# Local attention layers on one core: inverse norms by logarithm, exponential and one Newton step for two chunks at a time, and the mask added by four 64x64 matmuls

## The reference, cut to what matters

```
def l2norm(t):
    return t / jnp.clip(jnp.linalg.norm(t, axis=-1, keepdims=True), 1e-12)
...
q = l2norm(q) * qs
k = l2norm(k) * ksc
q, k = rotary_xpos(q, k)
...
bq = q.reshape(b, h, w, WINDOW, d) * QK_SCALE          # WINDOW 64, 8 heads of 64
sim = jnp.einsum('bhwid,bhwjd->bhwij', bq, bk)          # bk: this window's and the one before it
mask = (i < j) | (i > j + WINDOW) | (j == -1)
sim = jnp.where(mask, -jnp.finfo(sim.dtype).max, sim)
attn = jax.nn.softmax(sim, axis=-1)
...
x = x + o @ wo
h = ((h - mu) / jnp.sqrt(var + 1e-05) * lg + lb) @ w1 + b1
a, g = jnp.split(h, 2, axis=-1)
x = x + (a * jax.nn.gelu(g, approximate=False)) @ w2 + b2
```

## Time and profile before

| | |
|---|---|
| median of 3 runs (lowest to highest) | 1306.38 us (1305.3 to 1306.8) |
| the profiled execution: time / span | 1305.02 / 1303.2 us |
| stage A, to the first mask matmul | 590.65 us |
| start of the first and of the last of the 64 steps | 590.65 and 1257.25 us |
| busy share PE, DVE, ACT, POOL | 92, 86, 74, 82% |
| mean granted TensorE clock | 0.984 |

### The profile page before, as it was taken

One profiled execution on the slowest core, in us unless ns is written; L12 is line 12 of the kernel. 1 busy time (PEld: TensorE's weight loads), 2 busy tenths in 40 slices (PEclk: granted clock), 3 DMA queues, 4 the chain that ended last, 5 costly groups with the idle time before them and its releaser, 6 DMA issues.

```text
span 1303.2 us, 37200 instructions
## 1 busy us (share of the span) xinstructions
PE 1200.7 (92%) x12352; PEld 984.2 (76%) x12352; DVE 1124.0 (86%) x2210; ACT 958.8 (74%) x1772; POOL 1070.0 (82%) x1431
## 2 busy tenths in 40 slices
PE   3799999999999999977899999999999999999975
PEld 2588888888888888865677777777777777777764
DVE  2799999999999999957888888888888988888873
ACT  3477777777777777655688878888887877787762
POOL 1877777777777777687999999999999999999962
PEclk9799999999999999998999999999999999999998
DMA  6000000000000000001121211112122111111110
GB/s 181 8 12 14 14 14 14 12 12 12 9 11 12 12 8 10 16 7 46 40 48 39 49 42 43 46 46 50 39 53 52 45 50 47 49 48 47 43 35 25
DMA packets 87053, 44.28 MB, mean 34 GB/s; under 512 B 43908, under 2 KB 80048, under 8 KB 86960
## 3 DMA queue, kind: packets, MB, share of 16 engines
q1 hardware_dynamic: 86960, 43.08, 12.9%
HBM read 19.99 MB, written 6.29 MB: 20 GB/s over the span
## 4 chain that ended last, share of the span: by engine, by line
PE 39%; POOL 32%; DVE 14%; issue 11%; SPq 2%; ACT 1%; POOLq 1%; DVEq 0%; DMA 0%; ACTq 0%
POOL rnorm L716 11%; POOL kT L705 9%; PE bank L1415 7%; PE bank L1382 6%; PE bank L1397 6%; POOL probs L766 4%; DVE sums L1083 4%; POOL kT L719 3%; PE bank L1357 3%; DVE probs L1100 2%; PE bank L1426 2%; PE bank L1533 2%; PE bank L1359 2%; PE bank L1512 2%; PE bank L1568 2%
## 5 line engine op out<-in xcount | busy, mean ns | idle before, releaser
L655 POOL TENSOR_TENSOR probs<-probs,coef 128x1024 f32<-128x1024 f32 x128 | 241.0, 1904 | 5.0
L716 POOL TENSOR_TENSOR rnorm<-norm,halves 128x8 f32<-128x8 f32 x128 | 213.8, 1671 | 10.7
L705 POOL TENSOR_TENSOR kT<-qT 128x512 f32<-128x512 f32 x128 | 164.0, 1281 | 7.2 <-DVE qT L1177 7.2
L1091 DVE TENSOR_REDUCE mx<-bank 128x8 f32<-128x512 f32 x256 | 162.8, 678 | 3.9 <-PE bank L1397 3.8
L1100 DVE TENSOR_TENSOR probs<-bank,mx 128x512 f32<-128x512 f32 x256 | 162.1, 675 | 0.1
L849 ACT ACTIVATE probs<-probs 128x1024 f32<-128x1024 f32 x128 | 135.2, 1056 | 35.7 <-DVE probs L1100 33.8
L1083 DVE TENSOR_REDUCE sums<-probs 128x16 f32<-128x1024 f32 x128 | 154.0, 1212 | 6.5 <-ACT probs L849 6.5
L1382 PE MATMUL bank<-ident,probs 128*128 128x128 f32 x1024 | 137.8, 278 | 10.1 <-ACT wT L843 7.4
L719 POOL TENSOR_TENSOR kT<-kT,rnorm 128x512 f32<-128x512 f32 x128 | 133.6, 1044 | 10.0
L843 ACT ACTIVATE wT<-bank 128x512 f32<-128x512 f32 x256 | 137.1, 589 | 0.5 <-PE bank L1382 0.5
L1382 PEld LDWEIGHTS bank<-ident,probs 128*128 128x128 f32 x1024 | 114.2, 142 | 26.0 <-issue 14.2
(11 more groups left out here) (130 smaller groups left out, 3107.8 us busy)
## 6 DMA issues: line engine op xcount, KB each, us to landing
probs<-f_v SPq DMA_DIRECT2D x96, 128.0 KB, 2.3
res<-stage_x SPq DMA_DIRECT2D x48, 128.0 KB, 3.8
xn<-in_x SPq DMA_DIRECT2D x16, 128.0 KB, 2.2
xr<-in_x SPq DMA_DIRECT2D x16, 128.0 KB, 2.1
stage_x<-xo SPq DMA_DIRECT2D x32, 64.0 KB, 1.6
hn<-stage_x SPq DMA_DIRECT2D x32, 64.0 KB
mn<-mid SPq DMA_DIRECT2D x64, 32.0 KB
stage_x<-yo SPq DMA_DIRECT2D x16, 128.0 KB, 2.1
```

Of the source, the lines that this page charges most:

```text
L655: nc.gpsimd.tensor_tensor(out=e[:, :, :, :], in0=e[:, :, :, :], in1=coef[r % 2][:, 2, A_REP * at:A_REP * (at + 1), :].unsqueeze(3).broadca ...
L705: nc.gpsimd.tensor_tensor(out=qk[m][:, :, :], in0=on_self[m % 2][:, :, :], in1=on_partner[m % 2][:, :, :], op=ALU.add).then_inc(added, 1)
L716: nc.gpsimd.tensor_tensor(out=rnorm[:, at], in0=norm2[:, 1, at], in1=halves[:, 0:F_HEADS], op=ALU.pow).then_inc(rnorm_set, 1)
L1091: nc.vector.tensor_reduce(mx[s % 2][:, 2 * k:2 * k + 2, :], banks[2 * (s % 2) + k][:, :].rearrange("p (h c k) -> p h c k", h=2, c=CHUNKS), ...
```

## The change

The inverse norm is made in another way, on other engines and for two chunks (128x16) at once. ACT squares 2x instead of x, so that the sum is four times the squared norm s. POOL guards it, once for two chunks. ACT takes Ln, then Exp with a scale of -0.5: an r near s^-0.5. POOL makes one Newton step of four small operations, (3 - s r r) r, and multiplies both chunks one after the other. ACT's table loads are written out by hand: one set that holds both functions is loaded at the start of the step of tile 1, after the Gelus. Ln, Exp, the Newton step and the two products stand at the start of the step after the one in which the chunks were made, where chunk 0 or 2 was before multiplied in the step itself. PE's two transposes of chunks (and ACT's copies of them) move later in the step. The mask is added by four matmuls 64x64 (one for each corner of the array) instead of two 128x128, with a semaphore increment on PE ahead of them that carries the waits.

```diff
                 def squares(index, local, m, turn):
...
-                    nc.scalar.activation(sq[m % 2][:, :], f_bank("qk", local, turn)[:, :], ACT.Square).then_inc(squared, 1)
+                    nc.scalar.activation(sq[m % 2][:, :], f_bank("qk", local, turn)[:, :], ACT.Square, scale=2.0).then_inc(squared, 1)
...
+                def roots_near(unit, tile):
+
+                    at, j = slice(2 * F_HEADS * tile, 2 * F_HEADS * (tile + 1)), TILES * unit + tile
+                    act.wait_ge(guarded, j + 1)
+                    wait(act, root_near, j - 1)
+                    nc.scalar.activation(root[:, 0, at], norm2[:, 1, at], ACT.Ln).then_inc(log_set, 1)
+                    act.wait_ge(log_set, j + 1)
+                    wait(act, root_step, ROOT_STEPS * (j - TILES + 1))
+                    nc.scalar.activation(root[:, 1, at], root[:, 0, at], ACT.Exp, scale=-0.5).then_inc(root_near, 1)
...
+                        if tile == 1 and f_exists(turn, s - 1, F_LATE["gates"]) and f_exists(turn, s):
+                            load_log_and_exp()
+                        if prepares(turn, p, tile) and not (turn == "first" and s == 0):
+                            roots_near(unit + tile, 1 - tile)
                         if tile == 1 and prepares(turn, p, 2):
                             rounded(it, p + 2, turn)
...
-                    nc.gpsimd.tensor_scalar_max(norm2[:, 1, at], norm2[:, 0, at], NORM_FLOOR).then_inc(guarded, 1)
...
-                    nc.gpsimd.tensor_tensor(out=rnorm[:, at], in0=norm2[:, 1, at], in1=halves[:, 0:F_HEADS], op=ALU.pow).then_inc(rnorm_set, 1)
...
+                    nc.gpsimd.tensor_tensor(out=root[:, 2, at], in0=root[:, 1, at], in1=root[:, 1, at], op=ALU.mult).then_inc(root_step, 1)
+                    pool.wait_ge(root_step, k + 1)
+                    nc.gpsimd.tensor_tensor(out=root[:, 2, at], in0=root[:, 2, at], in1=norm2[:, 1, at], op=ALU.mult).then_inc(root_step, 1)
+                    pool.wait_ge(root_step, k + 2)
+                    nc.gpsimd.tensor_tensor(out=root[:, 2, at], in0=threes[:, 0:2 * F_HEADS], in1=root[:, 2, at], op=ALU.subtract).then_inc(root_step, 1)
+                    pool.wait_ge(root_step, k + 3)
+                    wait(pool, qk_normed, 2 * (j - TILES) + 2)
+                    nc.gpsimd.tensor_tensor(out=rnorm[:, at], in0=root[:, 2, at], in1=root[:, 1, at], op=ALU.mult).then_inc(root_step, 1)
...
+                        if prepares(turn, p, tile) and not (turn == "first" and s == 0):
+                            normalise(unit + tile, 1 - tile)
                         if prepares(turn, p):
                             sums(4 * (unit + 1) + 2 * tile, 2 * tile)
-                            normalise(unit + 1, 2 * tile)
...
                             sums(4 * (unit + 1) + 2 * tile + 1, 2 * tile + 1)
-                            normalise(unit + 1, 2 * tile + 1)
+                            guarded_norms(4 * (unit + 1) + 2 * tile + 1, tile)
...
-                    for k in range(2):
-                        nc.tensor.matmul(banks[k][:, :].rearrange("p (a k) -> p a k", a=4), ident16[:, :],
-                                         mask[:, tile, :].unsqueeze(1).broadcast_to([P, 4, F_KEYS]), start=True, stop=False)
+                    pe.sem_inc(scores_waited, 1)
+                    for w in range(2):
+                        for k in range(2):
+                            lo = F_HD * k
+                            nc.tensor.matmul(banks[k][WINDOW * w:WINDOW * (w + 1), :].rearrange("p (a k) -> p a k", a=4),
+                                             ident16[lo:lo + WINDOW, lo:lo + WINDOW],
+                                             mask[lo:lo + WINDOW, int(tile + w > 0), :].unsqueeze(1).broadcast_to([WINDOW, 4, F_KEYS]),
+                                             start=True, stop=False)
...
+                        if follows:
+                            weighted_values(it, late, late_s // TILES, late_s % TILES)
                         if prepares(turn, p, tile):
                             if follows:
                                 pe.wait_ge(eT_read, 2 * late + 2)
                             ahead("qkT", 4 * (p + tile) + 2 - 2 * tile)
-                        if follows:
-                            weighted_values(it, late, late_s // TILES, late_s % TILES)
                         following("values")
+                        if prepares(turn, p):
+                            ahead("v", TILES * (p + 1) + tile)
                         if prepares(turn, p, tile):
                             pe.wait_ge(f_read["qkT"], 4 * (unit + tile) + 3 - 2 * tile)
                             ahead("qkT", 4 * (p + tile) + 3 - 2 * tile)
-                        if prepares(turn, p):
-                            ahead("v", TILES * (p + 1) + tile)
```

More of the change, by code:

```diff
@@ new lines, in normalise @@
+                def normalise(unit, tile):
+                    at, j = slice(2 * F_HEADS * tile, 2 * F_HEADS * (tile + 1)), TILES * unit + tile
+                    k = ROOT_STEPS * j
+                    pool.wait_ge(root_near, j + 1)
+                    pool.wait_ge(guarded, j + 1)
+                    nc.gpsimd.tensor_tensor(out=root[:, 2, at], in0=root[:, 1, at], in1=root[:, 1, at], op=ALU.mult).then_inc(root_step, 1)
[6 more added lines that the diff above has]
+                    nc.gpsimd.tensor_tensor(out=rnorm[:, at], in0=root[:, 2, at], in1=root[:, 1, at], op=ALU.mult).then_inc(root_step, 1)
+                    pool.wait_ge(root_step, k + 4)
+                    for m in range(2 * tile, 2 * tile + 2):
+                        pool.wait_ge(added, 4 * unit + m + 1)
+                        nc.gpsimd.tensor_tensor(out=qk[m][:, :, :], in0=qk[m][:, :, :],
+                                                in1=rnorm[:, F_HEADS * m:F_HEADS * (m + 1)].unsqueeze(2).broadcast_to([P, F_HEADS, F_HD]),
+                                                op=ALU.mult).then_inc(qk_normed, 1)
@@ L1012, in body @@
                             squares(4 * (unit + 1) + 2 * tile + 1, 4 * (p + 1) + 2 * tile + 1, 2 * tile + 1, turn)
-                        if prepares(turn, p, tile):
-                            transposed(unit + tile, 4 * (p + tile) + 2 - 2 * tile, 2 - 2 * tile, turn)
                         if f_exists(turn, s, F_ATT_LAG):
@@ L1682, in score_mask @@
     within = (key >= q % WINDOW) & (key <= q % WINDOW + WINDOW)
-    first = within & ((q >= WINDOW) | (key >= WINDOW))
+    first = within & (key >= WINDOW)
     return np.where(np.concatenate([first, within], axis=1), 0.0, MASKED).astype(np.float32)
```

45 lines of the change are left out of this document (28 added, 17 removed).

## The result

| | before | after |
|---|---|---|
| median of 6 runs each (lowest to highest) | 1306.59 us (1305.3 to 1307.05) | 1310.72 us (1309.06 to 1312.45) |
| the profiled execution: time / span | 1305.02 / 1303.2 us | 1309.06 / 1307.3 us |
| mean granted TensorE clock | 0.984 | 0.990 |
| first mask matmul (boundary) | 590.65 us | 589.27 us, -1.4 (forecast -1.2) |
| filling, 8 steps | 81.0 us | 73.5 us, -7.5 (forecast -8.3) |

The changed kernel is slower by a little, but clear of the noise: the ratio of the times is 1.0034, with a 95% interval from 1.0021 to 1.0046. The forecast was 1286 us, with a range of 1264 to 1303. The stretches of the table are distances of mask matmuls in the two profiled executions; they add up, but for rounding, to the +4.1 us between the spans. The two layers hold the whole error, 15.8 + 10.0 us.

The account below looks back on a forecast made before the run. POOL was taken to set the pace of both layers. First layer +3.5, second layer -13.8, filling -8.3 and boundary -1.2 made -19.8 us from the 1306.4 us median: 1286.6, say 1286 us, range 1264 to 1303.

Parts of the forecast that it names:

- POOL's side: POOL in both layers: 5.2 us less per unit, to 15.5 and 17.1 us, so it stops being the bound.
- The mask: Mask matmuls on PE: four overlapping corners gain 0.2 us in the step of tile 0, nothing in that of tile 1.
- Step of tile 0: PE paces this step by itself: 9.64 us less 0.2 gives 9.44 us.
- ACT's detour in the step of tile 1: Table load, Ln and Exp delay ACT's rounded input by 1.78 us, to +4.53; DVE stalls 0.43 us.
- the rival of the drained load: ACT's table load before Ln costs a second such length as drain: +35 us, 1321 us; chance 0.06.
- The failed step: Step of tile 1: DVE's rows after the stall run on without a gap, so the step takes 11.48 us.
- A second term of the same kind: Second layer: DVE's closing normalisation fits into its waits for scores, 0.86 us, so it adds nothing.
- The filling: Eight steps that fill the pipeline before the first layer: 81.0 us falls to 72.7, a gain of 8.3 us.
- the boundary: PE's 8.51 us wait for POOL's four chunks and pads before the steps: a gain of 1.2 us, 0 to 4.
- serial corners: Slower rival: PE's four mask corners run one by one at full latency, 1.2 us; 1325 us, chance 0.05.
- a longer detour on ACT: Slower rival: load before Ln costs over 1.28 us, each 0.1 us costing 2.75; from 0.72 no gain; chance 0.06.
- The faster case: Rival: ACT's chain is shorter and PE bounds at 19.5 us a unit; 1247 us, or 1270 if half; chance 0.15.

Follow-up runs that it names:

- hc first: The changed kernel with DVE making hc ahead of the low part instead of behind the early product; 1277.14 us, ratio 0.9787 to the kernel before.
- hc with two tensors: The changed kernel with hc made by scalar_tensor_tensor, the inverse deviation as a broadcast second tensor; 1295.69 us, ratio 0.9926 to the kernel before.

## Why the prediction was wrong, step by step

- **POOL's side: right.** Busy time fell by 162 us (forecast 160), its rows have brackets, and PE no longer waits for the softmax's weights (26.9 us in 29 waits before).
- **The mask: right.** Four corners take 0.41 us together, and the first score matmul starts 0.24 us behind the first corner (forecast 0.3, before 0.52). The wait has moved ahead of the mask, as forecast: the corners' weight load has 0.37 us of "issue" ahead of it, and the scores' load, which waited 0.42 us, has none. Corners and whole tiles differ by 0.25 us a unit (forecast 0.2).
- **Step of tile 0: right to 0.13 us,** 9.57 against 9.44 (9.50 outside the loop).
- **ACT's detour in the step of tile 1: right.** The table load takes 1.28 us (as before), Ln and Exp 216 ns each (forecast 210), the low part starts at +4.51 (forecast +4.53). DVE's stall is 0.67 us where 0.43 was written: its maxima start 1.36 us behind the mask and not 1.70, mostly by the mask's gain, which the forecast had left out of this step, and it so waits longer for the same input. (The 0.43 us of stall went into the forecast's sum as 0.45, a slip of 0.02.) ACT's rows behind the Gelus, which end at 828.39:

```profile
828.41 1.28 ACT L943 ACT_TABLE_LOAD   x1
829.71 0.21 ACT L951 ACTIVATE root<-norm 128x16 f32<-128x16 f32 x1
830.03 0.22 ACT L954 ACTIVATE root<-root 128x16 f32<-128x16 f32 x1
830.16 0.37 ACT L959 ACTIVATE fhT_high<-bank 128x256 fp32r<-128x256 f32 x1
```

  No second length of a load stands in them, so the rival of the drained load did not come.
- **The failed step** is the one sentence "From there DVE has no gap until it ends the late products (829.97 to 835.41 ...)", out of which came "the step takes 11.48 us". The DVE rows of before were shifted by 0.45 us with their lengths of before. Inside that stretch stand hc's two instructions, for which the prediction had no row. They measured 1.42 instead of 0.51 us, the step 12.46 instead of 11.48. Counted from mask to mask, the 27 steps of tile 1 in the two layers are 25.2 us longer than forecast. In them hc's rows take 38.6 us, where 27 rows of 0.59 us are 15.9: 22.6 us of the 25.2. A second term of the same kind stood at nothing: in the second layer the closing normalisation's work was taken to fit into DVE's waits. There zo is stretched beside POOL too (about 0.92 instead of 0.34 us for the first of two) and the step takes 12.62 us, 0.16 more than in the first, in all 1.8 us. The 28 steps of tile 0 are 1.6 us longer than forecast, and 1.0 us goes off because the forecast counted 11.5 units where there are 12 steps of tile 0 and 11 of tile 1: 25.8 us, the error of the two layers. The filling was 0.8 us dearer than forecast, the boundary and the last 46 us together 2.7 cheaper, which leaves 23.9 of the 24.7 us between the forecast and the median.
- **The rivals.** The slower case had two mechanisms (serial corners, a longer detour on ACT), and it was neither. "Wrong would be the prediction if ..." named neither DVE nor POOL's new place in time. Moving POOL's products from one place to another was costed on POOL and on those who read the chunks; what stands beside them at the new place was not looked at. The faster case, PE as the bound with 19.5 us a unit, did not come either: no unit of the first layer is shorter than 20.6 us in any run. It had taken all 0.78 us of the weight load's wait off PE's time, where the matmul row behind that load waits 0.34 us.
- **The sign was in the trace of before.** In the eight steps of filling hc once stood beside one of POOL's sums, and was stretched nearly threefold; DVE, then POOL:

```profile
643.37 1.55 DVE L1195 TENSOR_SCALAR hc<-mn,mmv,mrstd 128x128 f32<-128x128 f32 x2 [0.51 <-POOL mrstd L742]
```

```profile
643.30 1.28 POOL L705 TENSOR_TENSOR kT<-qT 128x512 f32<-128x512 f32 x1
```

  hc's group of before has a shortest instruction of 331 ns and a longest of 1291; such a spread in one form and one shape asks for a reason before its length is used.
- **With the collision gone the rest of the sum holds.** "hc first" has 331.6 and 237.9 us in the two layers, where the forecast was 334.7 and 240.6, and it ends at 1277 us. It is 9 us below the forecast, 5.8 of them in the layers: hc fills the stall of DVE, so that the step of tile 1 takes 11.19 us (11.35 in the second layer, where zo is still held up, 569 ns) and not 11.48. The rest lies ahead of the first mask (588.0 us) and behind the last (43.3 us).

The Trainium skill ("SBUF — State Buffer", SBUF: two separate sides) describes this: VectorE and GpSimd share a pair of ports as an exclusive lock, taken by whichever starts first for the whole instruction; on VectorE's side it names the modes that use both ports and instructions with two inputs in SBUF. This case's traces agree on the collision, in both directions: hc's 1.20 us end with POOL's product, and a POOL row of 0.22 us takes 0.38 beside hc with two tensors. No row shows in which mode hc's one-tensor form runs, nor that the first to start always wins, as said under "hc with two tensors". By that rule the collision could have been priced ahead; an estimate from the rows is up to the length of one product, 1.04 us, where 0.91 was measured (1.42 less 0.51). And "for the whole instruction" does not fit POOL's power, beside which hc is not held up, as the last section shows.

## What to carry to other kernels

When work is moved in time on POOL, list DVE's tensor_scalar and two-tensor instructions at the new place whose operands are all in SBUF, and price each at up to the full length of the POOL tensor_tensor beside it; the same for work moved on DVE. Reductions do not belong on that list, as the rows below show. Engine time that grows at an equal count of instructions can be a wait that the profile does not bracket: compare the shortest, mean and longest of one form. Where such a pair collides, put the small one ahead of the big one or let the big one wait for it (here 2.5% and 1.6% of the whole kernel), and before that look for a stall that it can fill.

## What the runs showed of the hardware that was not expected

- DVE's tensor_scalar and scalar_tensor_tensor of 128x128 in SBUF, some 0.33 us, take up to 1.21 us beside a POOL tensor_tensor of 128x512 of 1.04 us, and up to 1.29 beside one of 1.28 us (tensor_scalar), and up to 0.78 beside one of 128x256 (0.62 us).
- DVE's instructions that read PSUM (0.68 us for 128x512) keep their length beside the same POOL products: in the changed kernel the second product runs from about 832.7 to 833.7, and the two DVE products that stand there take 0.68 and 0.67 us.
- Operands in SBUF alone are not enough for a collision. DVE's reductions read SBUF and write SBUF, and keep their length: the softmax's sum over 128x1024 stands beside POOL's sum of 128x512 in 61 of the 64 steps of the changed kernel and takes 1.20 to 1.22 us in all of them. Before, then after, DVE and POOL (POOL's row of before is in the earlier trace rows, 833.65):

```profile
833.19 1.21 DVE L1277 TENSOR_REDUCE f_sum<-probs 128x8 f32<-128x1024 f32 x1
```

```profile
834.70 1.20 DVE L1321 TENSOR_REDUCE f_sum<-probs 128x8 f32<-128x1024 f32 x1
```

```profile
834.14 1.29 POOL L709 TENSOR_TENSOR kT<-qT 128x512 f32<-128x512 f32 x1 [0.43 <-DVE qT L1221]
```

- POOL's power of 128x8, 1.67 us long, does not hold hc up. In the trace of before it runs from 830.91 beside hc's two instructions (830.69 to 831.28), which take 0.59 us together. It is what stood beside hc in the step read, and the change put the products there. Whether a power of this size holds the ports for only a short part of its time was not measured.
